# Reading batch 1's expert results behind the last store of results, and computing the first turn's merge tiles later

## The reference

```python
x = x + tanh(g_xattn[0]) * L0_xattn(layernorm(x), ctx, ctx, ...)
x = x + tanh(g_ffn[0])   * L0_ffn(layernorm(x), ...)      # experts
x = x + tanh(g_xattn[1]) * L1_xattn(layernorm(x), ctx, ctx, mask, ...)
x = x + tanh(g_ffn[1])   * L1_ffn(layernorm(x), ...)

# the end of L0_ffn: perm is 1 where a token was chosen, else 0
result_permuted = einsum("bnesf,esdf->bnesd", inner, W2) + b2
result = einsum("bnesd,bntes->bntd", result_permuted, perm)

# attention: 16 heads of 32
scores = einsum("bhqd,bhkd->bhqk", q, k) / sqrt(32)
out = einsum("bhqk,bhkd->bhqd", softmax(scores), v)
```

## Time and profile before

| what | us |
|---|---|
| median of three runs | 1330.63 |
| lowest and highest run | 1325.4 and 1336.3 |
| the profiled execution as a run | 1328.46 |
| its span in the trace | 1326.7 |
| TensorE busy | 1258.9 (95%) |
| DVE, ACT, POOL busy | 885.8, 571.2, 554.4 |

### The profile page before, as it was taken

How to read it: one execution, slowest core, us unless ns; L and a number is a source line. 1 busy time by engine, 2 the same in 40 slices (tenths; PEclk the granted TensorE clock), 3 DMA queues, 4 the chain that set the end, 5 groups by cost and what they waited for, 6 DMA issues and landing times.

```text
span 1326.7 us, 28239 instructions
## 1 busy us (share of the span) xinstructions
PE 1258.9 (95%) x10607; PEld 906.3 (68%) x10607; DVE 885.8 (67%) x1570; ACT 571.2 (43%) x1039; POOL 554.4 (42%) x456
## 2 busy tenths in 40 slices
PE   8999999999999978887989999999998999999998
PEld 7777776777677667621447666766775778888887
DVE  6984787777676546663646766766675977777762
ACT  4345345434542545453562443353336433333331
POOL 3312642454251100000339657856734644444540
PEclk9999999999999979998999999999998999999999
DMA  9765455224411678999983643563323111111101
GB/s 350 225 179 187 154 159 174 101 88 149 141 73 36 208 217 257 321 400 354 400 348 93 222 170 97 174 220 132 121 84 128 64 63 63 63 43 52 63 27 37
DMA packets 126503, 213.59 MB, mean 161 GB/s; under 512 B 27610, under 2 KB 49370, under 8 KB 122332
## 3 DMA queue, kind: packets, MB, share of 16 engines
q1 hardware_dynamic: 126427, 212.57, 47.6%
HBM read 129.92 MB, written 82.62 MB: 160 GB/s over the span
## 4 chain that ended last, share of the span: by engine, by line
PE 77%; DVE 8%; DMA 5%; ACT 4%; issue 3%; SPq 3%; POOL 0%; ACTq 0%; DVEq 0%; POOLq 0%
PE b L157 12%; PE b L158 11%; PE b L159 11%; PE b L1586 5%; PE b L1784 5%; PE b L1785 5%; PE b L1786 5%; PE b L1558 4%; DMA s_rp<-e_chosen 3%; PE b L2080 3%; PE b L1691 3%; PE b L1699 3%; PE b L2098 2%; ACT a_pr L1150 2%; PE b L2114 2%
## 5 line engine op out<-in xcount | busy, mean ns | idle before, releaser
L1150 ACT ACTIVATE a_pr<-b 120x512 f32<-120x512 f32 x252 | 130.2, 603 | 95.1 <-PE b L1586 95.1
L1339 DVE TENSOR_REDUCE a_mx<-b 128x4 f32<-128x480 f32 x256 | 151.9, 651 | 10.4 <-PE b L1558 10.3
L1032 POOL TENSOR_TENSOR a_rp<-a_rp,a_b2s 128x512 f32<-128x512 f32 x96 | 120.5, 1296 | 23.8 <-DMA a_rp<-s_rp 23.8
L1071 POOL TENSOR_TENSOR a_atl<-a_pvs,a_ath 128x512 fp32r<-128x512 f32 x64 | 81.3, 1303 | 81.7 <-ACT a_ath L1194 81.7
L1784 PE MATMUL b<-a_woh,a_ath 128*128 128x512 f32 x256 | 104.6, 409 | 3.1 <-POOL a_atl L1071 3.1
L157 PE MATMUL b<-a_xth,a_wqh 128*128 128x512 f32 x256 | 104.2, 407 | 1.5 <-DVE a_xtl L1314 1.1
L158 PE MATMUL b<-a_xtl,a_wqh 128*128 128x512 f32 x256 | 101.6, 397 | 0.0
L159 PE MATMUL b<-a_xth,a_wql 128*128 128x512 f32 x256 | 101.6, 397 | 0.0
L1786 PE MATMUL b<-a_woh,a_atl 128*128 128x512 f32 x256 | 101.6, 397 | 0.0
L1785 PE MATMUL b<-a_wol,a_ath 128*128 128x512 f32 x256 | 101.5, 397 | 0.0
L1016 POOL TENSOR_TENSOR a_rstd<-a_ve,a_mhalf 128x4 f32<-128x4 f32 x16 | 16.2, 1014 | 190.9 <-DVE a_ve L1261 190.9
(11 more groups left out here) (245 smaller groups left out, 3142.4 us busy)
## 6 DMA issues: line engine op xcount, KB each, us to landing
a_rp<-s_rp SPq DMA_DIRECT2D x128, 256.0 KB, 4.5
s_x<-a_x SPq DMA_DIRECT2D x16, 1024.0 KB, 4.2
s_rp<-e_chosen SPq DMA_DIRECT2D x16, 1024.0 KB, 8.3
s_rp<-e_xc SPq DMA_DIRECT2D x16, 1024.0 KB, 8.4
e_w<-in_w SPq DMA_DIRECT2D x56, 256.0 KB, 4.8
a_xr<-in_x_t SPq DMA_DIRECT2D x8, 1024.0 KB, 6.6
a_x<-in_x SPq DMA_DIRECT2D x8, 1024.0 KB, 10.7
s_xn<-a_xn SPq DMA_DIRECT2D x8, 1024.0 KB, 4.7
```

What stands on the lines that cost most here:

```text
L1032: pool.tensor_tensor(rp[:, t, a], rp[:, t, a], b2s[:, :], ALU.add).then_inc(rp_biased, 1)
L1071: pool.tensor_tensor(quarter(atl, q), quarter(pvs, q), f(quarter(ath, q)), ALU.subtract).then_inc(a_lo, 1)
L1150: act.activation(pr[:, h % RING, :], bank[k][0:S2, :], ACT.Exp, scale=SCALE)\
L1339: dve.tensor_reduce(mx[:, t, :, r], bank[k][:, 0:HJ * S2].rearrange("p (a s) -> p a s", a=HJ), AX.X, ALU.max).then_inc(free[k], 1)
```

## The change

Two things are moved and nothing is added or taken away. In SP's list the reads of batch 1's `permb` and `a_rp` (17 DMAs, with the wait ahead of them) go from behind store 22 to behind store 31, the last (`EK - 1`). In TensorE's list for turn 0 alone, merge tiles 0 and 1 go behind scores 2, and merge tiles 2 and 3 behind values 1. The later turns stay as they were.

```diff
-        if u == 22:
+        if u == EK - 1:
             for k, uses in TW:
                 sp.wait_ge(full[k], uses.n(None, "merge", 1) + 1)
             load_perm(sp, 1)
@@
-            if merging:
+            late = merging and first_turn(i)
+            if merging and not late:
                 merge_tile(i, i + 1, 0)
                 merge_tile(i, i + 1, 1)
             scores(i, i, 1)
-            if merging:
+            if merging and not late:
                 merge_tile(i, i + 1, 2)
             values(0)
-            if merging:
+            if merging and not late:
                 merge_tile(i, i + 1, 3)
...
             scores(i, i, 2)
+            if late:
+                merge_tile(i, i + 1, 0)
+                merge_tile(i, i + 1, 1)
             values(1)
...
+            if late:
+                merge_tile(i, i + 1, 2)
+                merge_tile(i, i + 1, 3)
```

## The result

Over 19 runs each, on the same chips, the changed kernel took 1337.42 us in the median (1332.37 to 1341.51) and the kernel before 1330.56 (1325.4 to 1336.56). The ratio is 1.0052, with a 95% interval from 1.0037 to 1.0067, so the change costs 4.9 to 8.9 us, 6.9 in the middle. Forecast were +3.9 us, 1334.5, and a range of 1328 to 1342. It is slower, within 1%, as forecast, but by 3 us more than the sum.

A forecast was written before the change was run, and what follows sets the result against it. TensorE, busy 95% of the span, was taken as the bound. `a_xth` +3.6 us and `a_sums` +0.3, with the 1.14 us gain inside, gave +3.9: 1330.63 to 1334.5 us, range 1328 to 1342 (own range 1332 to 1338).

The forecast's parts named there:

- The bound and the sign: Whole kernel: TensorE is busy 95% of the span, so added pauses are kept; the change costs +3.9 us.
- The gain of 1.14 us: End of experts' results: copies stop waiting for slots, three TensorE waits go, scores 0 starts 1.14 us earlier.
- The new place of the reads: Behind the last store: 17.0 us until tile 3's last read lands, its results there at 690.9 us.
- Rival 1: Moved reads take 20.95 us, +7.9 us, or the clock falls oftener, +10 us: 1338 to 1341 us; chance 0.2.
- TensorE's new order: Turn 0: scores 1 starts some 2.1 us after scores 0; the list alone ends tile 3 4.6 us later.
- the clock: TensorE's half-speed stretches at new pauses and the spread: left out of the sum, priced at -1.2 to +2.4 us.
- Where the delay goes: Turn 0 behind tile 3, through DVE and ACT: `a_xth` 3.6 us later, the spread at 704.4 us.
- ACT's slack: Turn 0: the output weight's high part (2.19 us), formerly ahead of the transposed tokens, now fits into ACT's wait.
- POOL's list: POOL's turn 0 work comes 6.65 us later; `a_sums` then holds values 0 of turn 1, adding 0.3 us.
- The sum: Whole run: +3.6 + 0.3 = +3.9 us, the 1.14 us gain included; 1334.5 us on the median's scale.
- The fast side (2): Turn 0: moved tiles fit into slack, 1.14 us gain remains, 2.3 without low clock: 1328.3 us; chance 0.12.
- Rival 3: Last stores stay late: gain zero, the burst starts 1.14 us later, +5.0 us, 1335.7 us; chance 0.08.

The follow-up runs named there:

- the reads at store 26: Kernel before with the reads of batch 1 issued behind store 26 instead of store 22; ratio 1.0035 to the kernel before.
- before, again: The kernel before, unchanged, run again for a second trace; ratio 1.0016, spread of turn 1 at 108.45 us from the first query.

## Why the prediction was right or wrong, point by point

**The bound and the sign** were right. TensorE was 95% busy, the added pauses are in every trace of the changed kernel, and they aren't taken back later: from the spread of turn 1 to that of turn 7 the changed kernel needs 268.8 us and the kernel before 269.4. Behind that the traces of all kernels differ by up to 1.7 us, those of old and new order alike.

**The gain of 1.14 us** is the step that failed. Its mechanism was read rightly from the first trace: there the copies did wait for landing stores, and in the changed kernel the stores land early and no copy waits. But the waits of TensorE went only from 1.14 to 0.81 us. Two of 0.4 us remain that ACT's copies make with no store behind them; they are in every other trace. And in the second trace of before there was nothing to gain. Scores 0 is there at 36.80 us, and every other trace has it between 36.59 and 36.86, except the first of before (37.38) and that with the reads at store 26.

**The new place of the reads** was right in its main term: 17.2 us for 17.0. The burst began at 37.55 us for 36.6, since half of the gain was missing, even against the first trace, and `permb` took 0.80 us to issue and not 0.37. Rival 1's overfull queue (20.95 us) didn't come.

**TensorE's new order.** The pauses of 2.1 us ahead of scores 1 and 2.1 ahead of the transposes measured 2.18 and 2.38. The order was forecast to end tile 3 at 52.7 us after the first query if the reads cost nothing; with full clock it ended at 53.28, and the 0.6 us between are the gain that scores 0 lacked. With the clock as the chip granted it, it ended at 54.99. The second wrong step was to leave the clock out of the sum. It was priced at -1.2 to +2.4 us as if it could fall either way, and it doesn't: all four traces with the new order and unfilled pauses have half clock from scores 0 on, 6.8 us of it in three and 3.4 us in one. Of the six traces with the old order and the reads at store 22, two have it, for 3.4 us. The first trace of before has its half clock elsewhere, behind the spread.

**Where the delay goes.** DVE's 5.3 us were right (5.32), and so was ACT's slack (2.0 us, shown by moving the weight). From `a_xth` to the spread I took 6.34 us over unchanged from before; the changed kernel needed 7.1 and 7.7, with the half clock at the transposes. In all the spread of turn 0 was forecast for 67.1 us and came at 69.5 and 69.8. In the first of these traces the 2.4 us are 1.1 from tile 3, 0.5 from the transposes to `a_xth` and 0.8 behind it.

**POOL's list** was the right mechanism with the wrong size: +0.3 us. I took its slack, 94.48 - 91.72 = 2.76 us, from a trace in which the half clock behind the spread had delayed TensorE. In the second trace it is 92.56 - 91.35 = 1.2 us. In the changed kernel `a_sums` ends 8.1 and 7.4 us later than in the first trace of before, the tiles' whole delay of some 8 us, of which only this slack is taken off. TensorE waits 0.80 us for it in one trace; in the other it gets there by itself, 0.2 us behind `a_sums`. With the pauses filled or the weight moved it waits 0.79 us each time, so POOL's chain takes up what these edits could give.

**The sum.** The forecast was +3.9 us, run times say +6.9 (4.9 to 8.9), and spread 1 moved by 5.1 and 4.2 us against the first trace of before, by 7.6 and 6.8 against the second. In absolute terms the mark was forecast well: spread 1 at 110.97 + 3.9 = 114.9 us, measured 116.06 and 115.20. The larger part of the missing 3 us is thus the base. The trace that the forecast started from was 2.5 us slower in this stretch than its repetition, by a stretch of half clock and by late stores, and the forecast took the one for slack of POOL (1.5 us too much) and the other for a gain. Which of the two traces is the usual case isn't shown by two of them; the run times lie nearer to the second. So the sign and the chain were understood, and that 1337.4 lies within 1328 to 1342, and even within the forecast's own 1332 to 1338, owes something to the width of these ranges.

**The rivals.** The fast side (2) and the full 20.95 us (1) are refuted; of rival 1's half clocks two stretches came, mostly beside other waits. Rival 3, with its +5.0 us, has the number that comes near, but not for its reason: it said that the stores would stay late, and the last two land after 5.6 to 7.0 us instead of 8.3 to 8.4. Its argument was a misreading. The last two issues stand within 2.67 us in the changed kernel too (675.99, 2.67), where the queue is relieved, so that is the pace of the parts and not that of the queue. What came is that relieved stores gave TensorE little or nothing.

## What to carry to other kernels

Small stalls and slacks of one or two us shouldn't be read from a single trace: two executions of the same kernel differed by 2.5 us in a stretch of 111 us, and both the gain and the slack of this forecast were taken from one trace. A DMA that lands late is a cost only as far as somebody waits for it: here the stores came early and TensorE's waits stayed. A burst of reads costs little where the compute that waits for the stores is slow, and much directly ahead of a dense stretch or of its own consumer. Before independent work is moved, one should look for what it covers: here the merge tiles were the cover for the exponentials.

## What the runs showed of the hardware

In the first trace of the changed kernel the granted clock fell to one half 0.3 us behind the start of scores 0, after a pause of 1.68 us; in the second it fell in the pause of 2.2 us that follows scores 0. In both it stayed there for 6.8 us, through scores 1. In the same stretch with 16 unused matmuls in these two pauses TensorE kept the full clock. The first pause alone isn't always followed by it: of the six traces with the old order and the reads at store 22 two had half clock there, for 3.4 us. I hadn't expected filling to go with 2.1 us, nor that the gain would vanish wholly as soon as reads are in the way.

The queue, full behind the burst, drained by itself in under 20 us: stores issued right behind it landed after 11.2 to 16.0 us in before, again, and the last five after 6.4 to 7.8. In the changed kernel, without the burst ahead, the stores from 660.84 us on landed after 3.8 to 7.0.
